# A mixture-of-experts kernel: no clears between the scatters once the last dispatch is sent

## The reference

```
mod = silu(c) @ wmod                        # six rows per batch: sa, ca, ga, sb, cb, gb
h = layernorm(x) * (1 + ca) + sa
x = x + ga * attention(h)                   # 16 heads of 8, a band of at most 60 keys on each side
h = layernorm(x) * (1 + cb) + sb
score = relu(h @ rw1 + rb1) @ rw2 + rb2     # 8 experts, the best 2 of each token
gate = softmax(score, over the two chosen)
out = sum over e of gate[:, e] * (relu(h @ W1[e] + b1[e]) @ W2[e] + b2[e])
x = x + gb * out
```

## Time and profile before

| | |
|---|---|
| three runs | 534.79, 531.16, 533.98 us (median 533.98) |
| span of the profiled execution | 536.5 us |
| profiled span less the median | 2.5 us (0.5%) |
| clears on GpSimd | 128, 45.7 us busy, mean 357 ns |
| indirect transfers on GpSimd | 64 dispatches (mean 999 ns), 72 scatters (mean 1016 ns) |
| last dispatch of the profiled execution | starts at 400.00 us |
| last scatter | starts at 517.34 us |

### The profile page before, as it was taken

One profiled execution on the slowest core, in us unless ns is written; L12 is line 12 of the kernel. 1 busy time (PEld: TensorE's weight loads), 2 busy tenths in 40 slices (PEclk: granted clock), 3 DMA queues, 4 the chain that ended last, 5 costly groups with the idle time before them and its releaser, 6 DMA issues.

```text
span 536.5 us, 16755 instructions
## 1 busy us (share of the span) xinstructions
PE 453.1 (84%) x5323; PEld 356.0 (66%) x5323; DVE 378.4 (71%) x1026; ACT 349.0 (65%) x1521; POOL 369.7 (69%) x586
## 2 busy tenths in 40 slices
PE   6998888888888888887929996659668999999977
PEld 5565666666666666665504446658447999999977
DVE  6777999999999999999493565735332554555654
ACT  3668999999999999999523552424023787756800
POOL 6975655556688668764447879875888877777640
PEclk9999999999999999999876996969557999999979
DMA  9351000000000400301311121222211222224446
GB/s 236 83 172 46 13 12 13 13 12 13 14 13 12 111 14 14 91 12 44 99 44 34 51 83 51 81 70 79 91 60 61 80 71 82 69 81 137 133 135 194
DMA packets 61519, 36.54 MB, mean 68 GB/s; under 512 B 25806, under 2 KB 57334, under 8 KB 61306
## 3 DMA queue, kind: packets, MB, share of 16 engines
q1 hardware_dynamic: 55834, 25.83, 18.4%
q0 software_dynamic: 4352, 9.45, 5.2%
q10 hardware_dynamic: 1248, 0.20, 0.2%
HBM read 20.56 MB, written 14.88 MB: 66 GB/s over the span
## 4 chain that ended last, share of the span: by engine, by line
PE 35%; DVE 22%; ACT 21%; issue 12%; another core or an unknown queue 5%; POOL 2%; DVEq 2%; ACTq 0%; POOLq 0%
ACT pr L1026 20%; PE pAm L1935 9%; DVE nmax L1093 8%; PE pAm L1485 5%; PE pSpm L1943 5%; PE pScm L1943 4%; PE pScm L1255 2%; DVE oT L947 1%; PE pScm L1500 1%; DVE w1t L1793 1%; DVEq L1552 1%; PE pm L767 1%; DVE stat L1337 1%; PE pSpm L1492 1%
## 5 line engine op out<-in xcount | busy, mean ns | idle before, releaser
L1026 ACT ACTIVATE pr<-pS,nmax 128x136 f32<-128x136 f32 x512 | 185.5, 382 | 13.4 <-DVE nmax L1093 13.2
L1700 ACT ACTIVATE act<-pAm,w1t 128x128 f32<-128x128 f32 x288 | 82.6, 377 | 85.4 <-PE pAm L1935 41.2
L1026 ACT ACTIVATION_READ_ACCUMULATOR pr<-pS,nmax 128x1 f32 x512 | 108.8, 212 | 0.0
L1935 PE MATMUL pAm<-hgT,w1t 128*128 128x128 f32 x576 | 87.2, 293 | 19.3 <-issue 12.8
L1055 PE MATMUL pS<-kT,qbd 64*128 64x136 f32 x1024 | 93.8, 302 | 1.5 <-ACT pr L1026 1.2
L1935 PEld LDWEIGHTS pAm<-hgT,w1t 128*128 128x128 f32 x576 | 77.6, 206 | 24.7 <-issue 20.0
L1647 POOL DMA_INDIRECT y_scr<-ys,si x72 | 73.2, 1016 | 29.7 <-DVE ys L1809 18.0
L1093 DVE TENSOR_REDUCE nmax<-pS 128x4 f32<-128x544 f32 x128 | 87.6, 685 | 2.1 <-PE pS L1059 1.4
L1101 DVE STREAM_TRANSPOSE prT<-pr 128x640 f32<-128x640 f32 x96 | 81.1, 845 | 8.9 <-ACT pr L1026 0.2
L1055 PEld LDWEIGHTS pS<-kT,qbd 64*128 64x128 f32 x1024 | 68.3, 186 | 14.6 <-ACT pr L1026 1.1
L1614 POOL DMA_INDIRECT xs<-h_all,pos_i x64 | 64.0, 999 | 11.3 <-issue 9.6
(11 more groups left out here) (304 smaller groups left out, 716.4 us busy)
## 6 DMA issues: line engine op xcount, KB each, us to landing
hg<-xs SPq DMA_DIRECT2D x72, 72.0 KB
vbd<-v_scr SPq DMA_DIRECT2D x132, 16.0 KB, 1.7
v_scr<-h_all SPq DMA_DIRECT2D x8, 256.0 KB, 2.3
h_all<-y_scr SPq DMA_DIRECT2D x8, 256.0 KB, 3.1
w_all<-y_scr SPq DMA_DIRECT2D x8, 256.0 KB, 5.0
x_all<-in_L_attn_x SPq DMA_DIRECT2D x3, 512.0 KB, 6.1
w_all<-in_L_ffn_W SPq DMA_DIRECT2D x2, 768.0 KB, 4.9
w_all<-in_L_ffn_W SPq DMA_DIRECT2D x3, 512.0 KB, 5.1
```

Source lines behind the costliest of these rows:

```text
L1026: e.activation(pr[:, n, to:to + SPAN], scored(j, gi)[:, lo:lo + SPAN], ACT.Exp, bias=nmax[:, k:k + 1], scale=-1.0, accum_out=rs[u][:, k:k ...
L1700: e.activation(ac(u)[:, k, :], pU[u % W][:, k, :], ACT.Relu, bias=w1t[u // 2 % 4][:, u % 2, FF + D + k:FF + D + k + 1]).then_inc(a_up.sem, 1)
L1935: mm = e.matmul(pU[u % W][:, k, :], w1t[u // 2 % 4][:, u % 2, k * P:(k + 1) * P], hgT[u // 2 % 4][:, u % 2, :], start=True, stop=True)
```

## The change

Once the last dispatch and the scatter and clear that go with it are issued, the remaining scatters follow one another with nothing between them. Their number, order and waits are the same. 56 clears go, 72 remain.

```
                 for j in range(sent, NF):
                     scatter(j)
-                    if j < NF - 8:
-                        breath()
```

## The result

The changed kernel took 538.41 us (median of six, 534.81 to 541.59), the kernel before 532.22 us (median of six on the same chip). The ratio is 1.0118, its 95% interval 1.0079 to 1.0157: slower by a little over 1%, where I had forecast no change. On other chips the same edit turned out 2% faster, as the experiments show; both results have to be explained.

The account below looks back on a forecast made before the run. TensorE was taken to bound the steady stretch, with GpSimd off the path. Backlog 0 to -0.9 us, steady stretch 0, end 0, taken as -0.4: median 534.0 becomes 533.6 us, range of 8 in 10 529 to 541.

Parts of the forecast that it names:

- the backlog's term: From 403 us until GpSimd catches up near 415 us: scatters without clears end the kernel 0 to 0.9 us sooner.
- the steady stretch: From 420 us to beyond 495 us: TensorE is busy 15.00 of every 15.00 us, so removing clears gains 0.
- rival one: After 403 us: denser scatters prolong the other engines' starved state past 415 us; up to 15 us slower, half 7.6; 18%.
- What I held against rival one: From 415.83 to 435 us GpSimd is as full, yet TensorE runs 137 matmuls; last tiles' pairs without clears show no slowing.
- its one "for": The stretch after 403 us never had four such transfers in a row without clears; counted toward the 18% for slower.
- My sign of being right: In the profile after, TensorE still does 137 matmuls per 15 us from 420 us.
- has nobody to please: In the steady stretch no engine waits for GpSimd, so a scatter that leaves early gains nothing.
- 56 x 0.08 = 4.5 us: GpSimd's own time saved by removing 56 clears in a continuous stream, as each hides all but 0.08 us.
- The spacing without clears: From 403 us on, scatters were to start 1.37 us apart with pauses of 0.3 us.
- VectorE's copies: Copies of `w1t` in the steady stretch: at most 0.17 us shorter each, 9.5 us in all, hidden behind TensorE.
- The last scatter: At the kernel's end: to start at 517 us, give or take 1, as nothing moves there.

Follow-up runs that it names:

- e1_backlog: The changed kernel with clears put back behind the scatters of tiles 8 to 23 alone (16 of 56); 534.26 us on chip 1, ratio 1.0061.

## Why the prediction was wrong

**The step that failed** is the one that put the backlog's term of the sum at 0 to -0.9 us and the steady stretch's at 0, both because GpSimd was off the path. On chip 1 the clears of the backlog measured +0.34%, 1.8 us (0 to 3.6), and those of the tiles 24 to 63 +0.61%, 3.2 us (1.5 to 5.0). What the sum left out is shown for the backlog: on starved chips scatters that follow directly slow all other engines, TensorE among them, although GpSimd itself is off the path. From the last dispatch to GpSimd's first rest TensorE gets through 1.7 to 2.4 matmuls a us instead of 3.6 to 4.5 (25 in 15 us after the change, 34 in 19 without the backlog's clears and 26 in 11 on chip 10; 59 in 13 us, 64 in 18 and 96 in 24 with clears). The first result's two rows, before and then after:

```profile
402.00:415.00 13.00, 11.07 (x59) 9.65 (x59) 2.42 (x7) 4.52 (x17) 11.68 (x18) 0.76 0.18 58
```

```profile
403.00:418.00 15.00, 6.22 (x25) 4.45 (x26) 2.10 (x6) 2.83 (x10) 11.51 (x12) 0.73 0.19 62
```

That is rival one, which I gave 18%. The 538.4 us lie within my range of 529 to 541 only by that rival's share; my forecast proper, no effect at 531 to 537 us, does not hold them.

**Rival one's mechanism held, its price did not**: I had put 15 us, or 7.6 at half. I let the state last past 415 us up to 435. In fact it ends when GpSimd has run out of scatters, and without clears it runs out sooner. Twelve scatters take 15 us without clears, and TensorE then loses 15 x (1 - 1.7/9.1) = 12.2 us; with clears they take 17.4 us, and it loses 17.4 x (1 - 4.0/9.1) = 9.8 us. The difference, an estimate from these rows, is 2.4 us; with the other traces' rates it is anything from 0.5 to 3.5 (2.4 against 3.6 a us, 1.7 against 4.5). The kernel without backlog clears alone measured 0.34% of 531 = 1.8 us.

**What I held against rival one** was right as far as it went and weighed too much. A full GpSimd does not make the state by itself, as all three unstarved chips show. Whether pairs without a clear do harm is open: the trace of e1_backlog, where they follow directly from tile 24 on, has 586 matmuls from 435 to 500 us, as many as before, and yet that kernel is 0.61% slower. That I had seen the direct spacing only in pairs, and only at the end, was written down as its one "for", and it was the one that counted.

**The rest of the loss is open.** The first result is 6.2 us. The backlog explains about 2; the clears of tiles 24 to 63 are worth 3.2 us on chip 1, but no row of that kernel shows where. With both sets gone the steady stretch is no longer full: from 435 to 500 us TensorE did 586 matmuls before and 576 after, on chip 10 586 and 571. That is 10 and 15 x 15/137 = 1.1 and 1.6 us. My sign of being right, 137 in every 15 us, failed there, and nothing shows why. With the chip's noise of some 4 us within one kernel I can't place the remainder.

**That an early scatter "has nobody to please" was true of one kind of chip.** Where TensorE is starved at 375 to 415 us, it falls back to where GpSimd is, and GpSimd then waits for results. Where it is not, it is ten and more tiles ahead by the last dispatch, in the kernel before GpSimd never catches up, and its time from 403 us to the end is on the path. I had dismissed 56 x 0.08 = 4.5 us as GpSimd's own; the trace gives more. Between 1.45 us (with a full clear) and 1.27 us lie 0.18 us, 56 x 0.18 = 10 us, and a copy of VectorE in the way makes a clear 0.53 and not 0.32 us. The measured gain is 10 us on chip 9 (513.27 to 503.25) and 15 on chip 15 (520.12 to 505.24), by the medians.

**The spacing without clears** was 1.27 us, not 1.37; my pairs stood in the stretch where VectorE works most, and their instructions took 1.07 and not 0.97. **VectorE's copies** did get shorter (the median of the `w1t` copy, over the whole span, from 524 to 498 ns), hidden as forecast. **The last scatter** starts at 519.56 us, 2.2 us later than before and not within the 1 us that I had named.

**What makes a chip starved** stays open. Each chip was seen at one time only, so the chip and the state it was in at that time can't be told apart. Nor do the rows show what the engines wait for; in the first trace not one packet of an instruction queue moved from 380 to 396 us, but that may as well follow from their standing still, and it is no mark of the state: in the changed kernel two such packets moved from 403 to 419 us, as many as from 405 to 420 us on chip 9 at full pace.

No version beats both kernels on both kinds of chip. Unstarved, the changed kernel and the one with tiny clears are best (0.976 to 0.979); starved, no median was under that of the kernel before, though on chip 10 the changed kernel can't be told from it.

## What to carry to other kernels

A filler between transfers can be a price or a protection, and which one it is can differ from chip to chip; before costing its removal at nothing, look for stretches in which every other engine issues one instruction at a time for no named reason, and ask what GpSimd does there. An engine that waits for results in one trace may be the bound in another, so add up its whole queue from the stretch on and compare it with the pace of the bounding engine unhindered. And a ratio from one chip is a ratio from one chip: the same edit gave 1.012 and 0.976.

## What the runs showed of the hardware

Not expected: with indirect transfers starting 1.27 us apart for long, TensorE, VectorE and ScalarE came nearly to a standstill in the first result and on chips 1 and 10 (17, 7 and 7 matmuls in 15 us against 137) and were not touched on chips 9 and 15, nor on chip 6 with clears. On the first kind 0.17 us more between the starts of two transfers (1.45 against 1.28) was worth 25 us of 566, while pauses of 1.5 us and more took the effect away altogether (chip 1, 406 matmuls in 45 us). Why these chips differ is not shown.
